# Tile 2's layers placed ahead of tile 3's last gathered rows in a DLRM interaction kernel

## The reference

```python
e = jnp.stack([tbl_0[ids[:, 0]], ..., tbl_25[ids[:, 25]]], axis=1)   # 512 x 26 x 128
T = jnp.concatenate([r_dense[:, None, :], e], axis=1)                # 512 x 27 x 128
Z = jnp.einsum('bnd,bmd->bnm', T, T)
z = Z[:, iu0, iu1]                                                   # the 351 pairs n < m
h = jnp.concatenate([z, r_dense], axis=1)                            # 512 x 479
h = jnp.maximum(h @ W_top1 + b_top1, 0.0)                            # 512 x 512
h = jnp.maximum(h @ W_top2 + b_top2, 0.0)                            # 512 x 256
y = h @ W_top3                                                       # 512 x 1
```

## Time and profile before

| | |
|---|---|
| median of 3 runs | 124.29 us (123.7 to 124.66) |
| the profiled execution | 124.55 us, of it span 122.6 us |
| PE busy | 93.3 us (76%), 1460 matmul records |
| DVE, ACT, POOL busy | 75.5, 73.7, 75.4 us (60 to 62%) |
| chain that ended last: PE, POOL, issue, DMA, ACT, DVE | 10%, 8%, 5%, 3%, 3%, 1% |
| granted clock of PE, mean | 0.956 of full |

### The profile page before, as it was taken

The page is one execution under the profiler, slowest core; times in us unless marked ns, Lnnn a source line. Parts: engine busy times, 40 slices in busy tenths (PEclk is TensorE's granted clock), DMA queues, the critical chain, the costliest instruction groups (busy, mean ns, idle before and its releaser), DMA issues. The chain is left out here.

```text
span 122.6 us, 3575 instructions
## 1 busy us (share of the span) xinstructions
PE 93.3 (76%) x1460; PEld 76.8 (63%) x1460; DVE 75.5 (62%) x164; ACT 73.7 (60%) x154; POOL 75.4 (62%) x82
## 2 busy tenths in 40 slices
PE   5659988979789879956519798787947666579791
PEld 5547755646557658756408697676937456569680
DVE  4979999999999995036350993119920104880422
ACT  4097799998799978378380997209942105860000
POOL 4888777887887887787878787777878600040000
PEclk9999999999999999998555999999999999999999
DMA  1896786969899831121222122121222100000000
GB/s 50 244 311 214 259 262 203 289 184 275 184 241 345 267 85 43 43 70 47 66 61 70 50 67 62 51 64 48 64 62 65 48 21 5 8 19 1 0 5 0
DMA packets 7452, 13.64 MB, mean 111 GB/s; under 512 B 2378, under 2 KB 4108, under 8 KB 7308
## 3 DMA queue, kind: packets, MB, share of 16 engines
q1 hardware_dynamic: 5068, 8.67, 22.6%
q0 software_dynamic: 2368, 4.74, 14.3%
HBM read 13.16 MB, written 0.00 MB: 107 GB/s over the span
## 5 line engine op out<-in xcount | busy, mean ns | idle before, releaser
L301 POOL DMA_INDIRECT rows<-tbl,idx x72 | 73.3, 1018 | 22.9 <-issue 21.6
L353 PE MATMUL l<-hot,t_hi 128*128 128x512 f32 x68 | 29.4, 433 | 6.2 <-DVE hot L537 3.8
L537 DVE TENSOR_TENSOR hot<-ids_bc,rownum 128x512 fp32r<-128x512 int32 x51 | 32.3, 693 | 0.4 <-PE l L355 0.4
L355 PE MATMUL l<-hot,t_lo 128*128 128x512 f32 x68 | 28.1, 414 | 0.0
L419 DVE COPY Zlow<-gr 14x224 f32<-14x224 f32 x16 | 8.6, 540 | 22.2 <-PE gr L370 22.0
L353 PEld LDWEIGHTS l<-hot,t_hi 128*128 128x128 f32 x68 | 13.7, 201 | 13.5 <-issue 7.9
L370 PE MATMUL gr<-XT 128*32 128x26 f32 x1024 | 14.8, 202 | 8.4 <-issue 4.9
L370 PEld LDWEIGHTS gr<-XT 128*32 128x32 f32 x1024 | 12.7, 117 | 11.2 <-issue 7.0
L502 ACT COPY XT<-tp 128x512 f32<-128x512 f32 (+1 forms) x20 | 12.2, 654 | 10.6 <-PE tp L341 10.5
L341 PE MATMUL tp<-ident,rows 128*128 128x128 f32 x72 | 11.4, 295 | 7.4 <-DMA rows<-tbl,idx 3.7
L419 ACT COPY Zlow<-gr 14x224 f32<-14x224 f32 x16 | 8.7, 545 | 13.1 <-PE gr L370 12.9
(11 more groups left out here) (32 smaller groups left out, 62.5 us busy)
## 6 DMA issues: line engine op xcount, KB each, us to landing
ids_bc<-ids_oh SPq DMA_DIRECT2D x8, 256.0 KB, 4.1
table<-small SPq DMA_DIRECT2D x4, 512.0 KB, 4.1
table<-small SPq DMA_DIRECT2D x2, 640.0 KB, 5.6
rows<-tbl,idx POOLq DMA_INDIRECT x72, 3.2
w_sb<-w SPq DMA_DIRECT2D x1, 1024.0 KB, 8.6
table<-small SPq DMA_DIRECT2D x2, 320.0 KB, 5.4
w_sb<-w SPq DMA_DIRECT2D x1, 512.0 KB, 8.2
table<-small SPq DMA_DIRECT2D x2, 192.0 KB, 4.9
```

Of the source, the lines that this page charges most:

```text
L301: nc.gpsimd.indirect_dma_start(rows[:, t, place - FIRST, :], None, tbls[f], bass.IndirectOffsetOnAxis(ap=idx[:, t, f:f + 1], axis=0)).then ...
L353: nc.tensor.matmul(lookup_bank(i), t_hi[:, i % PARTS, c * D:(c + 1) * D], hot[:, k % HOTS, :], start=c == 0, stop=False)
L355: last = nc.tensor.matmul(lookup_bank(i), t_lo[:, i % PARTS, c * D:(c + 1) * D], hot[:, k % HOTS, :], start=False, stop=c == n - 1)
L537: nc.vector.tensor_tensor(hot[:, k % HOTS, :], ids_bc[:, i % IDS, :], rownum[:, v, c:c + 1].broadcast_to((OH_ROWS, BATCH)), ALU.is_equal). ...
```

## The change

In STEPS, layer 1 and layer 2 of each tile move forward. Layers of tile 0 come apart from each other and around the second gram half of tile 1; both halves of layer 1 of tile 1 now stand before the first gram half of tile 2, and layer 2 of tile 1 between the two gram halves of tile 2; layer 1 and layer 2 of tile 2 stand before the last rows of tile 3. What is left behind the last gram half is tile 3's own layers. Tile 3's layer 1 uses two `gr` banks and the two `tp` banks, so that its dense part waits for older copies only. Its four ReLUs alternate between DVE and ACT, and of the two L567 of tile 3 one goes to ACT and reads another bank.

```diff
-    steps += [("rows", 1, 0), ("rows", 1, 1), ("gram", 0, 0), ("gram", 0, 1), ("rows", 1, 2), ("gram", 0, 2),
...
+    steps += [("gram", 1, 0), ("rows", 2, 0), ("layer1", 0, 0), ("gram", 1, 1), ("layer1", 0, 1), ("rows", 2, 1),
+              ("layer2", 0, 0), ("rows", 2, 2), ("layer1", 1, 0), ("rows", 2, 3), ("layer1", 1, 1), ("rows", 2, 4)]
+    steps += [("gram", 2, 0), ("layer2", 1, 0), ("gram", 2, 1), ("rows", 3, 0), ("rows", 3, 1), ("layer1", 2, 0),
+              ("rows", 3, 2), ("layer1", 2, 1), ("layer2", 2, 0), ("rows", 3, 3), ("rows", 3, 4)]
+    steps += [("gram", 3, 0), ("gram", 3, 1), ("layer1", 3, 0), ("layer1", 3, 1), ("layer2", 3, 0)]
...
+def by_both(t, u):
+
+    return t == TILES - 1 and u % 2 == 1
+
+
 def units_ready(t, u):
 
-    return t + 1 + (u if t == TILES - 1 else 0)
+    if by_both(t, u):
+        return u // 2 + 1
+    return t + 1 + (u // 2 if t == TILES - 1 else 0)
...
-            return gr[:].rearrange("p k q n -> p (k q n)")[:, u * BANK:u * BANK + P]
+            if u < GRAM_BANKS - HALVES:
+                return gr[:, u, :, :].rearrange("p q n -> p (q n)")[:, 0:P]
+            return tp[:, u - (GRAM_BANKS - HALVES), 0:P]
+
+        def l2_block(t, v):
+
+            if t == TILES - 1 and v:
+                return gr[:, GRAM_BANKS - HALVES, :, :].rearrange("p q n -> p (q n)")[:, 0:P]
+            return l2[:, v * P:(v + 1) * P]
...
                 elif kind == "layer1" and t == TILES - 1 and i == 0:
-                    pe.wait_ge(gram_dve, HALVES * TILES)
-                    pe.wait_ge(gram_act, HALVES * TILES)
+                    pe.wait_ge(gram_dve, HALVES * t)
+                    pe.wait_ge(gram_act, HALVES * t)
+                    pe.wait_ge(tp_empty, banks)
                     for u in range(BLOCKS):
                         from_dense(t, u)
                 elif kind == "layer1" and t == TILES - 1:
+                    pe.wait_ge(gram_dve, HALVES * TILES)
+                    pe.wait_ge(gram_act, HALVES * TILES)
                     pe.wait_ge(low_in[t], 16 * (MOVES - SHARED_MOVES))
...
-                    pe.wait_ge(h2_ready, PIECES * (t + 1))
+                    pe.wait_ge(h2_ready, PIECES * t + (1 if t == TILES - 1 else PIECES))
+                    if t == TILES - 1:
+                        pe.wait_ge(h2_act, 1)
...
+                elif kind == "layer1" and t == TILES - 1 and i == 1:
+                    act.wait_ge(l2_full, t)
+                    for u in range(1, BLOCKS, 2):
+                        act.wait_ge(l1_full, t + 1 + u)
+                        nc.scalar.activation(h1[:, u, :], l1_block(t, u), ACT.Relu).then_inc(h1_act, 1)
+                elif kind == "layer2" and t == TILES - 1:
...
+                    nc.scalar.activation(h2[:, 1, :], l2_block(t, 1), ACT.Relu,
+                                         bias=tail_sb[:, 0, 1:2]).then_inc(h2_act, 1)
```

More of the change, by code:

```diff
@@ L100, in timeline @@
         steps += [("rows", 0, g) for g in ROWS_AFTER.get(i, [])]
-    steps += [("rows", 1, 0), ("rows", 1, 1), ("gram", 0, 0), ("gram", 0, 1), ("rows", 1, 2), ("gram", 0, 2),
[L102 to L111, removed]
+    steps += [("rows", 1, 0), ("rows", 1, 1)]
+    steps += [("gram", 0, 0), ("rows", 1, 2), ("gram", 0, 1), ("rows", 1, 3), ("rows", 1, 4)]
+    steps += [("gram", 1, 0), ("rows", 2, 0), ("layer1", 0, 0), ("gram", 1, 1), ("layer1", 0, 1), ("rows", 2, 1),
[3 more added lines that the diff above has]
+    steps += [("gram", 3, 0), ("gram", 3, 1), ("layer1", 3, 0), ("layer1", 3, 1), ("layer2", 3, 0)]
+    return steps
 STEPS = timeline()
@@ L216, in dlrm_tower @@
         l1_full, h1_ready, l2_full = sem("l1_full"), sem("h1_ready"), sem("l2_full")
+        h1_act, h2_act = sem("h1_act"), sem("h2_act")
         h2_ready, l3_full, y_ready = sem("h2_ready"), sem("l3_full"), sem("y_ready")
@@ L404, in _ @@
                         for u in range(BLOCKS):
-                            pe.wait_ge(h1_ready, units_ready(t, u))
-                            last = nc.tensor.matmul(l2[:, v * P:(v + 1) * P], w2_sb[:, u, v * P:(v + 1) * P],
+                            if by_both(t, u):
+                                pe.wait_ge(h1_act, units_ready(t, u))
+                            else:
+                                pe.wait_ge(h1_ready, units_ready(t, u))
+                            last = nc.tensor.matmul(l2_block(t, v), w2_sb[:, u, v * P:(v + 1) * P],
                                                     h1[:, u, :], start=u == 0, stop=u == BLOCKS - 1)
                     last.then_inc(l2_full, 1)
-                    pe.wait_ge(h2_ready, PIECES * (t + 1))
+                    pe.wait_ge(h2_ready, PIECES * t + (1 if t == TILES - 1 else PIECES))
+                    if t == TILES - 1:
+                        pe.wait_ge(h2_act, 1)
                     for v in range(PIECES):
@@ L505, in _ @@
                     banks += 1
+                elif kind == "layer1" and t == TILES - 1 and i == 1:
[4 more added lines that the diff above has]
+                elif kind == "layer2" and t == TILES - 1:
+                    act.wait_ge(w2_in, 2 * 16)
+                    act.wait_ge(l3_full, t)
+                    act.wait_ge(l2_full, t + 1)
+                    nc.scalar.activation(h2[:, 1, :], l2_block(t, 1), ACT.Relu,
+                                         bias=tail_sb[:, 0, 1:2]).then_inc(h2_act, 1)
         @block.vector
@@ L555, in _ @@
                     else:
-                        for u in range(BLOCKS):
-                            dve.wait_ge(l1_full, units_ready(t, u))
+                        for u in range(0, BLOCKS, 2):
+                            dve.wait_ge(l1_full, t + 1 + u)
                             nc.vector.tensor_scalar(h1[:, u, :], l1_block(t, u), 0.0, None,
@@ L565, in _ @@
                     dve.wait_ge(l2_full, t + 1)
-                    for v in range(PIECES):
-                        nc.vector.tensor_scalar(h2[:, v, :], l2[:, v * P:(v + 1) * P], tail_sb[:, 0, v:v + 1], 0.0,
+                    for v in range(PIECES if t < TILES - 1 else 1):
+                        nc.vector.tensor_scalar(h2[:, v, :], l2_block(t, v), tail_sb[:, 0, v:v + 1], 0.0,
                                                 ALU.add, ALU.max).then_inc(h2_ready, 1)
```

## The result

The changed kernel took **137.68 us** (median of 4 runs, 137.04 to 138.31) against 124.47 before: ratio 1.107, 95% interval 1.099 to 1.115. The profiled execution took 137.79, its span 135.9; the span grew by 13.3 us, from 122.6.

The account below looks back on a forecast made before the run. Gathers, then tile 3's chain with tile 2's leftover work, bound the end; 9.6 us late less 3.5 saved gave 130.65, plus 4.3 for the clock 134.95, or 134.7 against the median; range 129.3 to 138.8.

Parts of the forecast that it names:

- (a): From 66.95: rows, half of tile 0's layer 1, tile 1's second gram half, to 71.65; ReLU ends at 75.6.
- (b): Layer 2 of tile 0 follows from 75.65 and is done at 78.9.
- (c): Row groups and all of tile 1's layer 1 come ahead of tile 2's gram, whose first half starts at 85.4.
- (d): L567 waits behind copies on DVE; tile 2's second gram half runs 91.8 to 93.7, 8.5 us late.
- (e): From that half's end, low-part copies, DMA issues and landing take 6.5 us; PE idles 5.4; tile 2's layer 1 starts at 100.2.
- (f): Tile 2's layers 1 and 2, then tile 3's last rows; tile 3's gram starts at 111.1, 9.6 us late.
- The end: From tile 3's gram start to the last y copy: 16.1 us in place of 19.58, saving 3.5 at full clock.
- The factor of 1.75: Assumed slowdown of dense matmuls in layers 1 and 2 at the low clock, between 1.5 and 2.
- the clock terms: Low clock behind long pauses: +1.7 in tile 2's layer 1, +2.1 in the part from Zt, +0.5 in (d); sum +4.3.
- the first (full clock): Rival: same tile 2 chain, but the pauses leave the clock up, giving 130.4 us; chance 0.22.
- the second (faster): Rival: tile 3's gram starts less than 3.5 us late, tile 2's second half ending by 87.6, so faster; chance 0.05.
- the third (no change): Rival: lateness of 3.5 to within 1.2 us, the half ending near 87.6, so no change; chance 0.03.

Follow-up runs that it names:

- e4c: Changed kernel with layer 2 of tile 1 moved behind tile 2's second gram half and two groups of rows, short lookup: 132.5 us, ratio 1.059.
- e6: Changed kernel plus unread matmuls in PE's two long pauses (10 before tile 2's layer 1, 7 behind tile 3's dense part), long lookup: 201.26 us, ratio 1.084.
- r1: Changed kernel again, unaltered, beside the kernel before: 136.32 us against 124.06, ratio 1.099.
- e2: Kernel before with the changed kernel's order of steps, banks and ReLUs as before, long lookup: 201.8 us, ratio 1.079.
- e3b: Repeat of e3, long lookup again: 194.89 us, 68.6 us from lookup end to last y copy.
- e1: Changed kernel with the whole order of steps of before, long lookup: 188.8 us against 187.67.
- e3: Order of before with only tile 2's layers moved ahead of tile 3's last two row groups, plus the change's end, long lookup: 194.64 us, ratio 1.039.
- e4: Changed kernel with layer 2 of tile 1 moved behind tile 2's second gram half and two row groups, long lookup: 198.84 us, ratio 1.055.
- e4b: Same kernel as e4 on another chip, long lookup: 192.79 us.
- e5b: Order of before with only the second half of tile 2's layer 1 ahead of tile 3's last rows, plus the change's end, short lookup: 122.71 us, ratio 0.985.

## Why the prediction was right

The direction, the place and most of the size held, 134.7 forecast against 137.68 (136.32 in the second set of runs). Step by step, predicted and seen in the trace:

- (a), (b): layer 2 of tile 0 to be done at 78.9; 79.97. The low stretch of the clock in the lookup's wake lasted to about 69.7 and not to 67.5, which is 0.9 of it; the sum had this stretch at full clock.
- (c): tile 2's first gram half at 85.4; 86.16.
- (d): L567 behind the copies, seen as forecast (91.78). Second half at 91.8; 92.67. **Mis-sized: its end.** 93.7 was forecast, 96.81 seen, since PE stood 2.23 us inside the half, with releaser "issue". The 0.5 forecast for the clock here didn't come: the granted clock is 0.99 from 94 to 97. The prediction had weighed the "issue" pause only for tile 3's gram, where the row of before shows it, and the end kept it there (1.92).
- (e): 6.5 us from this end to layer 1; 96.81 to 103.33, 6.5. PE stood still for 4.75 of them, not 5.4, since its transposes ran at the low clock. e4c shows the cause: with layer 2 of tile 1 out of (d), 4 to 5 us come back.
- (f): from layer 1 to tile 3's gram 10.9 at full clock and 1.7 for the clock, 12.6; 103.33 to 115.80, 12.5. So the gram is 14.3 late, where the forecast had 9.6 + 2.2 for the clock.
- The end: -3.5, and +2.1 for the clock in the part from Zt. Seen: -1.0. The dense part is hidden and runs behind the gram, the part from Zt starts at 9.74 after the gram (9.95), and takes 5.25 in place of 2.78, +2.5. e6 gives the 2.5 us back. The ReLUs on two engines gave nothing, as forecast. The 0.3 for two L567 (L599 on DVE, L536 on ACT) in parallel didn't come: each took 0.35 to 0.37 and not 0.31, and from layer 2 to the last y copy it is 3.63 us, 3.64 before.
- The factor of 1.75 for dense matmuls at the low level is 3.55 / 2.25 = 1.6 for half a layer 1, and 1.9 for the part from Zt.

Summed: 13.3 us seen, 10.4 forecast; the missing 2.9 are the pause in (d) 2.2, the longer low stretch in (a) 0.9, and 0.4 of the end, less the 0.5 for the clock in (d) and 0.1 in (f). The pause is the largest and differs by execution: in r1 it is 1.27, tile 3's gram is 12.7 late and the span 11.8 longer, 1.4 over the forecast.

Where the account failed is the cause of the two falls of the clock. They were laid to the pauses of 5.4 us in (e) and 3.2 us in the end; by the stretches above the clock fell at 97 and at 121, each time over a microsecond before that pause began, and in r1 at 92 and at 119, before its pauses from 97.11 and 120.96. The pauses then went by at the low level, and what followed them ran at it for as long as forecast. e2, e3b and e6 show that such a pause can bring the fall by itself when the clock is still up, so the clock terms might have come about the way forecast, but in this kernel they did not: that 1.7 and 2.1 add up to the 3.8 us seen (1.3 and 2.5) is in part luck. What made the clock fall in either place isn't shown.

The three rivals fell: the first (full clock) by the 0.50 rows, the second (faster) and the third (no change) since the half ended at 96.8, 9 us past the 87.6 that they needed. Of the changed order's 16.7 us (e2 over e1), tile 2's layers ahead of the last rows account for some 6 (e3, e3b) and the place of tile 1's layer 2 for 5 (e4, e4b); how the rest divides among the other moves and the clock no run separates.

## What to carry to other kernels

An order that all engines follow couples them: a step moved for PE's sake also moves its short vector instructions, and behind a row of copies such an instruction holds PE in the middle of its layer. So look at each engine's own neighbours of the moved step, and at what starts from the step that is now late, here a chain of five DMAs that had always been hidden. Work that is taken off the end pays only where it goes into a wait that is there already; here the change's end with one half-layer moved, into a wait of 1 us for a gather, won 1.5%, and moving all of tile 2's layers, and those of the tiles before it, lost 10%.

## What the runs showed of the hardware

- Within streams of gram matmuls (10 to 15 ns a record) PE stood still for up to 2.5 us with releaser "issue", and a transfer of 16 KB on the instruction queue lay just ahead of two of these pauses: at 103.0 to 103.25 us in the kernel before (pause from 103.48) and at 94.0 to 94.25 in the changed one (pause from 94.27). In each kernel the place moved with the number of instructions ahead: in tile 3's gram behind record 206 in the kernel before, 170 in the changed one (36 records more ahead of it) and e4c, 190 in e5b (16 more), 150 in e6 (20 more than the changed one). That it is a boundary of PE's instruction stream is inferred from this.
- A dense part's matmul record from XT took 0.24 us and one from Zt 0.12, at the same size (1.98 us for 8 in the earlier trace rows, 2.94 for 24 in the earlier trace rows).
- In eight of the twelve runs the lookup stage grew from 51 us to 115 to 124 us. In e1 DVE waited 61.5 us there in 5 waits, the longest 20.4, for a releaser that the profile gives as "remote", each time before an instruction that reads the ids, most of it while the indirect gathers ran. That copies of ids and tables landed late is inferred; the cause is open.
